# Gated delta-rule attention and top-1 column FFN: the key-product rows laid out by halves for their broadcast, four transfers per half in place of eight

## The chip, the core and the metric

The kernel runs on one core of one Trainium2 chip. The metric is the device time of one execution in microseconds. All arithmetic is in 32-bit floats.

## What is computed

A block of attention with a recurrent state, then a column-routed feed-forward layer, both with layer norms and residuals, over x of shape (4, 2048, 512), with 16 heads of 32 channels. The part that matters here is the recurrence over time:

```
def step(S, inp):
    k_t, q_t, v_t, beta_t, a_t = inp
    S = S * a_t[..., None, None]
    kv_mem = jnp.einsum('bhd,bhde->bhe', k_t, S)
    delta = (v_t - kv_mem) * beta_t
    S = S + k_t[..., :, None] * delta[..., None, :]
    y_t = jnp.einsum('bhd,bhde->bhe', q_t, S)
    return (S, y_t)
```

Each delta depends on all earlier ones of its head. The feed-forward layer sends every token to the best of 16 columns (a 512x128 and a 128x512 product with a gelu between), which needs the tokens sorted by column.

## The kernel before, in words

**Tiling.** The 2048 time positions are cut into 32 tiles of T=64 (all 4 batches at once, 256 tokens), and each tile into NC=2 chunks of C=32 positions. Channels lie on the partitions: 4 groups of 4 heads (HP=4, 32 partitions a head), times 4 batches, make G=16 groups in the free dimension. One `step` of each engine's program works on three tiles at once: `chain` is the recurrence of the present tile, `ahead` the projections, norms and decays of the next, `after` the output projection, the routing and the residuals of the last. The loop body of PE, DVE, ACT and POOL holds two such steps and runs 15 times, with two steps before it and two behind it; SP's loop body holds one step. The order within a step is written out by hand for each engine, and semaphores tie the engines together. A second loop behind this one does the sorted column products.

**The recurrence in a chunk.** Within a chunk the deltas solve a triangular system. Its matrix is Ak: the key products of the chunk times the decay between the two positions (`decay_products`, line 1187 of the profile, on DVE). DVE solves it in two halves of CS=16 positions (`solve_half`). For each of 15 positions t0 of a half it multiplies the known delta into a row of the matrix (line 1213, into Ut) and takes it off the later positions (line 1216), each as two instructions of 8 groups. This is done with all 32 channels of a head on their partitions, so a row of the matrix, which belongs to a head, must stand on all 32 partitions of it. That is done by DMA: SP writes Ak to `pair_rows` in DRAM (line 303), waits until it has landed (line 305), and reads it back broadcast over 32 partitions, head by head, into `pairs[0]` and `pairs[1]`, one buffer for each half (line 312). POOL multiplies `pairs` by beta (`pairs_times_beta`, line 997) and DVE waits for that at line 1204. The second half of a chunk also needs the first half's deltas through PE (`first_half_to_u`, line 456).

**Names.** I write (c,j) for half j of chunk c. POOL multiplies in the order (0,1), (1,0), (1,1) and then (0,0) of the next tile. DVE frees `pairs[j]` at the end of a solve, and SP fetches the next half into it then. PE's other work of a step is mostly 128x128 products (lines 402, 510, 518). `state_to_u` (line 446, waits for the state S at 445) opens a step on PE; `add_to_state` (line 1228) closes it on DVE.

Before, `fetch_pairs(c)` did a whole chunk with all the transfers of both halves:

```
sp.dma_start(pair_rows[c].rearrange("h s r -> (h s) r"), Ak[c][:].rearrange("p t g -> p (t g)")).then_inc(s["rows_out"], 16)
...
for s0, t0 in PIECES:
    for h in range(HP):
        rows = pair_rows[c, h, j * CS + s0:j * CS + s0 + PIECE, (j * CS + t0) * G:(j + 1) * CS * G]
```

`PIECES` is [(0, 0), (8, 8)]: the matrix of a half is triangular, so rows 8 to 15 are read for positions 8 to 15 only.

Of the kernel before, what the change touches and what calls it, by code (L numbers as in the profile page):

```python
# [15 lines left out]
H, DH = 16, 32  # L16
# [28 lines left out]
PIECE = CS // 2  # L45
PIECES = [(0, 0), (PIECE, PIECE)]


TURNS = [
    ("xT", 0), ("xT", 1), ("qk", 0), ("rms", 0), ("alpha",), ("qk", 1), ("rms", 1), ("ss", 0),  # L50
    ("wo", 0), ("wo", 1), ("qk", 2), ("ss", 1), ("G", 0), ("G", 1), ("qk", 3),
    ("ss", 2), ("gate", 0), ("ss", 3), ("gate", 1), ("beta", 0), ("xfT", 0), ("xfT", 1), ("beta", 1), ("hid",),
    ("v", 0), ("logits",), ("v", 1), ("rank",)]
# [20 lines left out]
def sandwich_kernel(nc, x, w_in, wa, dt_bias, a_log, norm_w, wo, bo, col_emb, gw1, gb1, gw2, gb2,  # L74
                    w_cols, b_cols, proj_w, proj_b, ln_g, ln_b,
                    c_sq, c_sel, c_mask, c_iota, c_pad, c_tok, c_row, c_col, out, xs_dram):
    with ExitStack() as ctx:
# [57 lines left out]
        Ak = [sb(f"Ak{c}", [P, C, G]) for c in range(NC)]  # L135
# [4 lines left out]
        pairs = [sb(f"pairs{j}", [P, CS, CS, G]) for j in range(2)]  # L140
# [32 lines left out]
        sel_flat = pairs[0][:].rearrange("p s t g -> p (s t g)")  # L173
# [21 lines left out]
        def in_qr(*shape, dt=F32):  # L195
# [40 lines left out]
            pr_ready Ak_ready rows_out kkq_full kkq_free A_ready kt_ready kd_ready kqd_ready  # L236
# [9 lines left out]
        m_xs, m_wc = ([sem(f"{n}{u}") for u in range(MQ)] for n in ("m_xs", "m_wc"))  # L246
        pairs_free, pairs_in = ([sem(f"{n}{j}") for j in range(2)] for n in ("pairs_free", "pairs_in"))
# [19 lines left out]
        pair_rows = nc.dram_tensor("pair_rows", (NC, HP, C, C * G), F32, kind="Internal").ap()  # L267
# [21 lines left out]
        def _(sp):  # L289
# [10 lines left out]
            def fetch_pairs(c):  # L300
                sp.wait_ge(s["Ak_ready"], 1)
                sp.sem_inc(s["Ak_ready"], -1)
                sp.dma_start(pair_rows[c].rearrange("h s r -> (h s) r"), Ak[c][:].rearrange("p t g -> p (t g)")).then_inc(s["rows_out"], 16)
                sp.wait_ge(s["rows_out"], 16)
                sp.sem_inc(s["rows_out"], -16)
                for j in range(2):
                    sp.wait_ge(pairs_free[j], 1)
                    sp.sem_inc(pairs_free[j], -1)
                    for s0, t0 in PIECES:
                        for h in range(HP):  # L310
                            rows = pair_rows[c, h, j * CS + s0:j * CS + s0 + PIECE, (j * CS + t0) * G:(j + 1) * CS * G]
                            sp.dma_start(pairs[j][DH * h:DH * h + DH, s0:s0 + PIECE, t0:CS, :].rearrange("p s t g -> p s (t g)"),
                                         rows.unsqueeze(0).to_broadcast([DH, PIECE, (CS - t0) * G])).then_inc(pairs_in[j], 16)

# [15 lines left out]

            load_tokens(0)
            load_tokens(1)
            fetch_pairs(0)
            fetch_pairs(1)
            load_tokens(2)
            fetch_pairs(0)
            with sp.Fori(0, NT - 3) as i:
                load_residual(i)
                fetch_pairs(1)
                load_tokens(i + 3)  # L340
                store(i)
                fetch_pairs(0)
            load_residual(NT - 3)
            fetch_pairs(1)
            load_tokens(NT - 1)
            store(NT - 3)
            fetch_pairs(0)
            load_residual(NT - 2)
            fetch_pairs(1)
            store(NT - 2)  # L350
            load_residual(NT - 1)
            store(NT - 1)
# [36 lines left out]
        def _(pe):  # L389
# [59 lines left out]
            def first_half_to_u(c, half):  # L449

                if not half:
                    pe.wait_ge(s["A_ready"], 1)
                    pe.sem_inc(s["A_ready"], -1)
                    pe.wait_ge(s["delT_ready"], 1)
                    pe.sem_inc(s["delT_ready"], -1)
                on_tiles(half, "corr_full", lambda g, q, q_half: pe.matmul(  # L456
                    uk[q, g, CS:C], delT[c][q_half, g, :], Ak[c][q_half, CS:C, g],
                    start=False, stop=True, skip_group_check=True))
# [93 lines left out]
            def step(p, chain, after, ahead):  # L552

# [39 lines left out]

                if chain:
# [20 lines left out]

# [22 lines left out]

# [97 lines left out]
        def _(act):  # L738
# [86 lines left out]
            def step(p, chain, after, ahead):  # L825
# [5 lines left out]
                if ahead:  # L831
# [12 lines left out]

# [10 lines left out]
                if ahead:  # L855
# [18 lines left out]
                def next_gate(hp):  # L874
                    act.wait_ge(s["sg_free"], 1)
                    act.sem_inc(s["sg_free"], -1)
                    link(sigmoid("gate", hp, sg[:]))
                    act.sem_inc(s["gate_ready"], 1)

                if ahead:  # L880
                    next_gate(0)
# [8 lines left out]
                if ahead:  # L890
                    next_gate(1)

                def next_beta(hp):
                    link(sigmoid("beta", hp, flat(unit(beta, hp))))
                    act.sem_inc(bank_free("beta", hp), 1)
                    act.sem_inc(s["beta_ready"], 1)

                if ahead:
# [3 lines left out]
                    next_beta(0)  # L902
# [3 lines left out]
                if ahead:  # L906
                    next_beta(1)
# [12 lines left out]

# [53 lines left out]
        def _(pool):  # L974
# [15 lines left out]
            def pairs_times_beta(c, j):  # L990

                pool.wait_ge(pairs_in[j], 16 * HP * len(PIECES))
                pool.sem_inc(pairs_in[j], -(16 * HP * len(PIECES)))  # L993
                for t0 in range(CS - 1):
                    a = pairs[j][:, t0, t0 + 1:CS, :]
                    t = c * C + j * CS + t0 + 1
                    ins = nc.gpsimd.tensor_tensor(a, a, beta[:, :, t:t + WID[t0]].rearrange("p g t -> p t g"), ALU.mult)  # L997
                ins.then_inc(s["pr_ready"], 1)

            def step(p, chain, after, ahead, added):  # L1000

# [6 lines left out]

# [7 lines left out]

# [20 lines left out]
                if ahead:  # L1037
                    for hp in range(2):
                        pool.wait_ge(s["gT_ready"], 1)
                        pool.sem_inc(s["gT_ready"], -1)  # L1040
                        d = flat(unit(dec, hp))
                        link(nc.gpsimd.tensor_tensor(d, gsb[hp], gT[hp], ALU.subtract))
                        dt = d.rearrange("p (n t) -> p n t", t=C)
                        link(nc.gpsimd.tensor_tensor(dt, dt, mask[:].unsqueeze(1).to_broadcast([P, GU * NC, C]), ALU.add))
                        pool.sem_inc(s["diff_ready"], 1)
# [13 lines left out]

# [91 lines left out]
        def _(dve):  # L1151
# [30 lines left out]
            def decay_products(c):  # L1182
# [4 lines left out]
                link(v.tensor_tensor(Ak[c][:].rearrange("p t g -> p g t"), kkq[:, :, 0, :], d, ALU.mult))  # L1187
# [5 lines left out]
            def solve_half(c, j):  # L1193
# [74 lines left out]
            def choose_columns():  # L1268
# [7 lines left out]
                dve.sem_inc(bank_free("logits"), 1)  # L1276
                dve.wait_ge(s["sig_ready"], 1)
# [12 lines left out]

                dve.wait_ge(s["e_ready"], 1)
# [22 lines left out]
            def step(p, chain, after, ahead):  # L1314
# [13 lines left out]
                if after:  # L1328
                    for hp in range(2):
                        normed_outputs(hp)  # L1330
# [11 lines left out]
                if after:  # L1342
                    for tb in range(TB):
                        dve.wait_ge(s["wo_full"], 1)
                        dve.sem_inc(s["wo_full"], -1)
                        link(v.tensor_tensor(y[:, tb, :], bank("wo", tb), bo_sb[:], ALU.add))
                        dve.sem_inc(bank_free("wo", tb), 1)
                        token_stats(y, tb)
# [5 lines left out]
                if ahead:  # L1354
                    for hp in range(2):
                        dve.wait_ge(s["g_copied"], 1)
                        dve.sem_inc(s["g_copied"], -1)
                        link(v.transpose(gT[hp], gsb[hp]))
# [201 lines left out]
```

## Time and profile before

| | before |
|---|---|
| time, median of 3 runs | 4272.6 us (4265.62 to 4274.22) |
| the profiled execution's own time | 4266.35 us |
| its span | 4264.5 us |
| busy share of the span | PE 75%, DVE 67%, POOL 48%, ACT 29% |
| granted TensorE clock, mean | 0.844 |
| DMA, mean | 91 GB/s |

Times are in us from the start of the span, durations of one instruction in ns where it says so. The two-step loop stands between about 190 and 3520 us; its iterations start some 222 us apart. In a row of the timeline, "[2.64 <-DVEq L1227]" says that the engine had sat idle for 2.64 us before the row and that the wait at line 1227 ended that. "<-issue" is idle time in which the engine waited for nothing that the profile shows. A row that merges n instructions has "xn" at its end; a 32-bit product of PE counts as two.

### The profile page before, as it was taken

To read this page: it belongs to the slowest core of one execution; us is meant where nothing else is said; L and a number is where in the kernel's file an instruction comes from. 1 tells how busy PE (TensorE), PEld (TensorE's weight loads), DVE (VectorE), ACT (ScalarE), POOL (GpSimd) and SP (SyncE) were. 2 spreads that over 40 slices of the span, in tenths; PEclk is the share of its full clock that TensorE was granted. 3 is DMA by queue.
4 is the path that set the end of the run, shared out by engine and by line. 5 is a ranking of instruction groups with operands and counts; after the bars stand their busy time and mean duration, and the time that the engine had idled before them with its cause. 6 is when DMAs were issued, how large, how long until landed. Compare 5 with 4: busy or idle time off the path is not lost. (4 is left out here: it accounts for less than half of the span.)

```text
span 4264.5 us, 151843 instructions
## 1 busy us (share of the span) xinstructions
PE 3206.8 (75%) x59364; PEld 2424.2 (57%) x59364; DVE 2863.6 (67%) x12347; ACT 1247.4 (29%) x2119; POOL 2051.5 (48%) x3051
## 2 busy tenths in 40 slices
PE   5787878888788888887888887888887885355553
PEld 4566656666566666666666666666666664233332
DVE  1676767777776767776777676767777776565655
ACT  2233333333333333333333233333333331111110
POOL 1444444444444444444444444444445443277776
PEclk9898888988888989888988898888898896677766
DMA  4444444433344444444434343434444442466663
GB/s 114 77 86 87 86 86 81 84 73 82 75 85 82 86 86 86 87 86 86 86 77 86 79 89 76 86 75 83 84 86 86 86 86 49 140 151 145 150 150 75
DMA packets 416983, 388.41 MB, mean 91 GB/s; under 512 B 42816, under 2 KB 346560, under 8 KB 415824
## 3 DMA queue, kind: packets, MB, share of 16 engines
q1 hardware_dynamic: 399696, 345.37, 38.0%
q0 software_dynamic: 16640, 33.71, 3.8%
q8 instruction: 492, 8.06, 0.8%
q14 instruction: 155, 1.27, 0.1%
HBM read 307.22 MB, written 75.93 MB: 90 GB/s over the span
## 5 line engine op out<-in xcount | busy, mean ns | idle before, releaser
L402 PE MATMUL work<-xT,w_sb 128*128 128x256 f32 x5120 | 1387.6, 421 | 122.9 <-PEq L393 101.8
L997 POOL TENSOR_TENSOR pairs<-pairs,beta 128x240 f32<-128x240 f32 (+14 forms) x1920 | 938.7, 529 | 982.2 <-POOLq L993 982.2
L402 PEld LDWEIGHTS work<-xT,w_sb 128*128 128x128 f32 x5120 | 1029.4, 209 | 337.1 <-issue 186.1
L1213 DVE TENSOR_TENSOR Ut<-pairs,uk 128x120 f32<-128x120 f32 (+14 forms) x3840 | 833.3, 255 | 25.6 <-DVEq L1204 20.9
L1216 DVE TENSOR_TENSOR uk<-uk,Ut 128x120 f32<-128x120 f32 (+14 forms) x3840 | 708.2, 226 | 0.0
L446 PE MATMUL uk<-kqd,S 32*32 32x32 f32 x8192 | 121.4, 216 | 243.5 <-PEq L445 186.5
L510 PE MATMUL work<-wo_sb,ctxT 128*128 128x512 f32 x512 | 269.6, 687 | 17.2 <-PEq L393 17.2
L1200 DVE TENSOR_TENSOR uk<-vT,uk 128x128 f32<-128x128 f32 x256 | 63.3, 293 | 311.2 <-DVEq L1320 186.2
L986 POOL TENSOR_TENSOR kqd<-kq,eg 128x1024 f32<-128x1024 f32 x64 | 150.5, 2352 | 231.4 <-POOLq L1053 231.4
L446 PEld LDWEIGHTS uk<-kqd,S 32*32 32x32 f32 x8192 | 106.5, 127 | 272.9 <-issue 272.4
L771 ACT ACTIVATE qraw<-work 128x512 f32<-128x512 f32 x128 | 75.9, 593 | 628.2 <-ACTq L770 628.2
L728 PE MATMUL kkq<-w_sb,kq 128*128 128x512 f32 x160 | 130.6, 913 | 104.3 <-PEq L727 104.3
L1034 POOL TENSOR_TENSOR x<-x,y 128x512 f32<-128x512 f32 x64 | 81.3, 1270 | 247.8 <-POOLq L1033 247.8
L510 PEld LDWEIGHTS work<-wo_sb,ctxT 128*128 128x128 f32 x512 | 110.9, 223 | 153.7 <-issue 152.5
L708 PE MATMUL work<-squares,w_sb 128*128 128x128 f32 x320 | 70.2, 367 | 166.7 <-PEq L706 166.4
L708 PEld LDWEIGHTS work<-squares,w_sb 128*128 128x128 f32 x320 | 51.7, 191 | 213.5 <-issue 213.3
L436 PEld LDWEIGHTS kkq<-kq 32*32 32x32 f32 x8192 | 135.3, 115 | 57.5 <-issue 57.5
L464 PE MATMUL uq<-kqd,S 32*32 32x32 f32 x8192 | 102.4, 200 | 83.5 <-issue 83.5
L1135 POOL DMA_INDIRECT out<-pairs,qr x80 | 130.0, 1624 | 72.3 <-POOL pairs L1133 33.7
L956 ACT ACTIVATE kq<-work 128x512 f32<-128x512 f32 x80 | 47.8, 597 | 387.4 <-ACTq L954 387.4
L436 PE MATMUL kkq<-kq 32*32 32x64 f32 x8192 | 156.9, 230 | 4.1 <-issue 4.1
L456 PEld LDWEIGHTS uk<-Ak,delT 16*32 16x32 f32 x8192 | 88.7, 113 | 117.8 <-issue 117.8
(190 smaller groups left out, 5637.7 us busy)
## 6 DMA issues: line engine op xcount, KB each, us to landing
pairs<-pair_rows SPq DMA_DIRECT2D x512, 256.0 KB, 5.0
pairs<-pair_rows SPq DMA_DIRECT2D x512, 128.0 KB, 6.3
w_sb<-xs_rows SPq DMA_DIRECT2D x80, 258.0 KB, 2.8
w_sb<-in_w_cols SPq DMA_DIRECT2D x80, 256.0 KB, 4.1
w_sb<-in_proj_w SPq DMA_DIRECT2D x80, 256.0 KB, 4.3
xt<-in_x SPq DMA_DIRECT2D x66, 256.0 KB, 3.8
pair_rows<-Ak SPq DMA_DIRECT2D x64, 256.0 KB, 2.0
x<-in_x SPq DMA_DIRECT2D x64, 256.0 KB
```

The lines of the kernel that those rows point to most:

```text
L402: mm = pe.matmul(w[:, half * BT:(half + 1) * BT], w_sb[:, f, j * D + hg * P:j * D + (hg + 1) * P], xT[:, f, :], start=(f == 0), stop=(f == ...
L436: on_tiles(half, "kkq_full", lambda g, q, q_half: pe.matmul(kkq[q, g], kq[q, g, c, 0, :], kq[q, g, c].rearrange("p a t -> p (a t)"), start ...
L446: on_tiles(half, "uk_full", lambda g, q, q_half: pe.matmul(uk[q, g], S[q, g, :], kqd[c][q, g, 0, :], start=(g == 0), stop=True, skip_group ...
L464: on_tiles(half, None, lambda g, q, q_half: pe.matmul(uq[q, g], S[q, g, :], kqd[c][q, g, 1, :], start=(g == 0), stop=True, skip_group_chec ...
L510: mm = pe.matmul(w, flat(ctxT[:, hg * B + tb * BL:hg * B + (tb + 1) * BL, :]), wo_sb[:, hg, :], start=(hg == 0), stop=(hg == KD - 1))
L708: mm = pe.transpose(m_tp[u % 2][:, f * P:(f + 1) * P], xs[u][:, f * P:(f + 1) * P], ident)
L728: pe.matmul(m_yp[u % 2], hm[u % 2], pw[u], start=True, stop=True).then_inc(s["m_y"], 1)
L986: link(nc.gpsimd.tensor_tensor(kqd[c][:], kq[:, :, c], eg[:, :, c * C:(c + 1) * C].unsqueeze(2).to_broadcast([P, G, 2, C]), ALU.mult))
L997: ins = nc.gpsimd.tensor_tensor(a, a, beta[:, :, t:t + WID[t0]].rearrange("p g t -> p t g"), ALU.mult)
L1135: nc.gpsimd.indirect_dma_start(out_rows, bass.IndirectOffsetOnAxis(ap=toki[:, u:u + 1].bitcast(U32), axis=0), z[u], None, bounds_check=ROW ...
L1213: link(v.tensor_tensor(Ut[:, g, 0:n], pr[:, g], uk[:, g, at:at + 1].to_broadcast([P, G // 2, n]), ALU.mult), behind=1)
L1216: link(v.tensor_tensor(uk[:, g, at + 1:at + 1 + n], uk[:, g, at + 1:at + 1 + n], Ut[:, g, 0:n], ALU.subtract), behind=1)
```

## The change

`Ak` is laid out as [half, group, position in the half] in place of [position, group]. `pair_rows` has a part for each half, in which the 16 rows of a head stand one behind the other with 16 x 16 floats each. So the 15 rows that a half needs are one run of 15 KB, and a head is one transfer of 32 partitions x 3840 floats: four transfers per half in place of eight. `PIECES` is gone: all 16 positions of all 15 rows are read. `pairs[j]` is [row, group, position]. The instructions that read or write `Ak` and `pairs` are the same in number and size with their strides exchanged. `rows_out` is a semaphore for each chunk. SP's program is written as one `step`, with the write of the rows apart from the two fetches.

```
-        Ak = [sb(f"Ak{c}", [P, C, G]) for c in range(NC)]
+        Ak = [sb(f"Ak{c}", [P, 2, G, CS]) for c in range(NC)]
-        pairs = [sb(f"pairs{j}", [P, CS, CS, G]) for j in range(2)]
+        pairs = [sb(f"pairs{j}", [P, CS, G, CS]) for j in range(2)]
-        pair_rows = nc.dram_tensor("pair_rows", (NC, HP, C, C * G), F32, kind="Internal").ap()
+        pair_rows = nc.dram_tensor("pair_rows", (NC, 2, HP, C, G * CS), F32, kind="Internal").ap()
...
-            def fetch_pairs(c):
+            def write_rows(c):
                 sp.wait_ge(s["Ak_ready"], 1)
                 sp.sem_inc(s["Ak_ready"], -1)
...
+                sp.dma_start(pair_rows[c].rearrange("j h s n -> (h s) j n"), Ak[c][:].rearrange("p j g t -> p j (g t)"))\
+                    .then_inc(rows_out[c], 16)
+
+            def fetch_pairs(c, j):
+                if not j:
+                    sp.wait_ge(rows_out[c], 16)
+                    sp.sem_inc(rows_out[c], -16)
+                sp.wait_ge(pairs_free[j], 1)
+                sp.sem_inc(pairs_free[j], -1)
+                for h in range(HP):
+                    rows = pair_rows[c, j, h, j * CS:j * CS + CS - 1, :].rearrange("s n -> (s n)")
+                    sp.dma_start(pairs[j][DH * h:DH * h + DH, 0:CS - 1].rearrange("p s g t -> p (s g t)"),
+                                 rows.unsqueeze(0).to_broadcast([DH, (CS - 1) * G * CS])).then_inc(pairs_in[j], 16)
...
+            def step(chain, after, ahead, block, following):
+
+                if chain:
+                    fetch_pairs(0, 1)
+                if after:
+                    load_residual(block)
+                if chain:
+                    write_rows(1)
+                    fetch_pairs(1, 0)
+                    fetch_pairs(1, 1)
+                if ahead:
+                    load_tokens(following)
+                if after:
+                    store(block)
+                if ahead:
+                    write_rows(0)
+                    fetch_pairs(0, 0)
...
                 for t0 in range(CS - 1):
-                    a = pairs[j][:, t0, t0 + 1:CS, :]
+                    a = pairs[j][:, t0, :, t0 + 1:CS]
                     t = c * C + j * CS + t0 + 1
-                    ins = nc.gpsimd.tensor_tensor(a, a, beta[:, :, t:t + WID[t0]].rearrange("p g t -> p t g"), ALU.mult)
+                    ins = nc.gpsimd.tensor_tensor(a, a, beta[:, :, t:t + WID[t0]], ALU.mult)
...
-                link(v.tensor_tensor(Ak[c][:].rearrange("p t g -> p g t"), kkq[:, :, 0, :], d, ALU.mult))
+                link(v.tensor_tensor(Ak[c][:].rearrange("p j g t -> p g j t"),
+                                     kkq[:, :, 0, :].rearrange("p g (j t) -> p g j t", j=2),
+                                     d.rearrange("p g (j t) -> p g j t", j=2), ALU.mult))
...
-                    pr = pairs[j][:, t0, t0 + 1:CS, :].rearrange("p t g -> p g t")
+                    pr = pairs[j][:, t0, :, t0 + 1:CS]
```

The rest of the diff writes loops out and splits functions; it leaves the other engines' instructions in their order.

SP's queue in its loop body and just behind it, before (Ak0 and Ak1 are the two chunks, pairs0 and pairs1 the two halves' buffers):

```order
L303 DMA pair_rows<-Ak0 128x512 [waits store_done,Ak_ready]
L312 DMA pairs0<-pair_rows 32x8x256 [waits rows_out,pairs_free0]
L312 DMA pairs0<-pair_rows 32x8x256 x3
L312 DMA pairs0<-pair_rows 32x8x128 x4
L312 DMA pairs1<-pair_rows 32x8x256 [waits pairs_free1]
L312 DMA pairs1<-pair_rows 32x8x256 x3
L312 DMA pairs1<-pair_rows 32x8x128 x4
L337 REGISTER_ALU
L337 COMPARE_AND_BRANCH
L319 DMA x1<-in_x 64x2x512 [waits x1_free]
```

The same place after:

```order
L304 DMA pair_rows<-Ak0 128x2x256 [waits store_done,Ak_ready]
L315 DMA pairs0<-pair_rows 32x3840 [waits rows_out0,pairs_free0]
L315 DMA pairs0<-pair_rows 32x3840 x3
L355 REGISTER_ALU
L355 COMPARE_AND_BRANCH
L315 DMA pairs1<-pair_rows 32x3840 [waits pairs_free1]
L315 DMA pairs1<-pair_rows 32x3840 x3
L322 DMA x1<-in_x 64x2x512 [waits x1_free]
```

Eight issues per half became four; the loop's branch moved from behind the fetch of (0,1) to ahead of it; each transfer follows the same ones as before.

DVE's queue behind the first solve of a step, before:

```order
L1220 STREAM_TRANSPOSE delT0<-uk 128x512 [waits dve_step]
L1323 STREAM_TRANSPOSE kd0<-kq 128x512 [waits dve_step]
L1323 STREAM_TRANSPOSE kd1<-kq 128x512 [waits dve_step]
L1187 TENSOR_TENSOR Ak1<-kkq,dec 128x16x32 [waits dve_step,kkq_full]
L1189 TENSOR_TENSOR Aq1<-kkq,dec 128x512 [waits dve_step]
```

And after:

```order
L1217 STREAM_TRANSPOSE delT0<-uk 128x512 [waits dve_step]
L1322 STREAM_TRANSPOSE kd0<-kq 128x512 [waits dve_step]
L1322 STREAM_TRANSPOSE kd1<-kq 128x512 [waits dve_step]
L1182 TENSOR_TENSOR Ak1<-kkq,dec 128x16x2x16 [waits dve_step,kkq_full]
L1186 TENSOR_TENSOR Aq1<-kkq,dec 128x512 [waits dve_step]
```

Nothing changed its place; the write of Ak has one more dimension.

## Rows read from the trace of the kernel before

**Rows 1.** The page's first line.

```profile
span 4264.5 us, 151843 instructions
```

**Rows 2.** The page's costliest groups: busy us, mean ns of one, idle before.

```profile
L997 POOL TENSOR_TENSOR pairs<-pairs,beta 128x240 f32<-128x240 f32 (+14 forms) x1920 | 938.7, 529 | 982.2 <-POOLq L993 982.2
L1213 DVE TENSOR_TENSOR Ut<-pairs,uk 128x120 f32<-128x120 f32 (+14 forms) x3840 | 833.3, 255 | 25.6 <-DVEq L1204 20.9
L1216 DVE TENSOR_TENSOR uk<-uk,Ut 128x120 f32<-128x120 f32 (+14 forms) x3840 | 708.2, 226 | 0.0
```

**Rows 3.** Groups by line, the two products of decay_products on DVE.

```profile
L1187 DVE TENSOR_TENSOR Ak<-kkq,dec 128x512 f32<-128x512 f32 x64 | 66.1, 1033 | 24.2 <-DVEq L1185 24.2
L1189 DVE TENSOR_TENSOR Aq<-kkq,dec 128x512 f32<-128x512 f32 x64 | 44.2, 691 | 9.4
```

**Rows 4.** The page's DMA issues: count, KB each, median us to landing.

```profile
pairs<-pair_rows SPq DMA_DIRECT2D x512, 256.0 KB, 5.0
pairs<-pair_rows SPq DMA_DIRECT2D x512, 128.0 KB, 6.3
```

**Rows 5.** Busy time in stretches; the last three columns are clock, DMA share, GB/s.

```profile
0.00:20.00 20.00, 0.00 (x0) 0.00 (x0) 0.00 (x0) 0.00 (x0) 0.18 (x4) 1.00 0.84 309
1723.00:1742.00 19.00, 13.55 (x190) 11.23 (x188) 10.98 (x48) 6.35 (x10) 7.79 (x16) 0.86 1.07 194
1767.50:1775.50 8.00, 4.74 (x217) 3.44 (x216) 5.60 (x22) 4.07 (x8) 3.50 (x3) 0.93 1.07 197
1784.00:1788.00 4.00, 4.00 (x16) 2.57 (x15) 3.09 (x6) 0.00 (x0) 0.82 (x4) 1.00 1.14 202
1788.00:1790.00 2.00, 2.00 (x10) 1.58 (x9) 1.66 (x11) 0.26 (x1) 0.00 (x0) 1.00 1.23 192
```

**Rows 6.** Timeline of SP's issues, two chunks of one step.

```profile
1722.60 8.98 SPq L312 DMA_DIRECT2D pairs<-pair_rows  x16
1766.54 19.37 SPq L312 DMA_DIRECT2D pairs<-pair_rows  x16
```

**Rows 7.** Timeline of PE over both steps of one loop iteration.

```profile
1745.15 0.54 PE L446 MATMUL uk<-kqd,S 32*32 32x32 f32 x22 [6.95 <-PEq L445]
1748.21 1.70 PE L446 MATMUL uk<-kqd,S 32*32 32x32 f32 x106 [2.52 <-issue]
...
1776.09 0.87 PE L464 MATMUL uq<-kqd,S 32*32 32x32 f32 x49 [3.85 <-issue]
...
1810.75 0.73 PE L456 MATMUL uk<-Ak,delT 16*32 16x16 f32 x64 [2.17 <-PEq L455]
...
1818.45 3.44 PE L402 MATMUL work<-xT,w_sb 128*128 128x256 f32 x8 [2.85 <-PEq L393]
...
1853.97 1.69 PE L446 MATMUL uk<-kqd,S 32*32 32x32 f32 x92 [4.95 <-PEq L445]
1857.36 0.74 PE L446 MATMUL uk<-kqd,S 32*32 32x32 f32 x36 [1.70 <-issue]
...
1900.37 0.49 PE L478 MATMUL su<-delT,kd 32*32 32x32 f32 x34 [2.76 <-issue]
...
1926.96 3.75 PE L402 MATMUL work<-xT,w_sb 128*128 128x256 f32 x8 [3.99 <-PEq L393]
```

**Rows 8.** Timeline of DVE in the same iteration.

```profile
1740.92 0.69 DVE L1228 TENSOR_TENSOR S<-Sd,su 128x512 f32<-128x512 f32 x1 [0.37 <-DVEq L1227]
...
1766.60 0.19 DVE L1246 TENSOR_TENSOR alog<-work,dtb 128x32 f32<-128x32 f32 x1 [1.57 <-DVEq L1245]
...
1792.85 0.69 DVE L1237 TENSOR_TENSOR kq<-qraw,qr 128x512 f32<-128x512 f32 x1 [2.44 <-DVEq L1236]
...
1901.13 0.69 DVE L1228 TENSOR_TENSOR S<-Sd,su 128x512 f32<-128x512 f32 x1 [2.64 <-DVEq L1227]
```

**Rows 9.** Timeline of POOL in the same iteration.

```profile
1732.60 7.23 POOL L997 TENSOR_TENSOR pairs<-pairs,beta 128x240 f32<-128x240 f32 x15 [26.01 <-POOLq L993]
...
1871.32 1.08 POOL L1012 TENSOR_TENSOR kd<-kd,dec 128x512 f32<-128x512 f32 x1 [1.38 <-POOLq L1010]
```

More of the change, by code:

```diff
@@ L246, in sandwich_kernel @@
         m_xs, m_wc = ([sem(f"{n}{u}") for u in range(MQ)] for n in ("m_xs", "m_wc"))
+        rows_out = [sem(f"rows_out{c}") for c in range(NC)]
         pairs_free, pairs_in = ([sem(f"{n}{j}") for j in range(2)] for n in ("pairs_free", "pairs_in"))
@@ L594, in step @@
                     first_half_to_u(0, 1)
-                if chain:
                     state_to_outputs(0, 0)
@@ L890, in step @@
                 if ahead:
[L891 to L898, printed above, removed]
+                    act.wait_ge(s["sg_free"], 1)
+                    act.sem_inc(s["sg_free"], -1)
+                    link(sigmoid("gate", 1, sg[:]))
+                    act.sem_inc(s["gate_ready"], 1)
                     if chain:
@@ L901, in step @@
                         act.sem_inc(s["vb_free"], -1)
-                    next_beta(0)
+                    link(sigmoid("beta", 0, flat(unit(beta, 0))))
+                    act.sem_inc(bank_free("beta", 0), 1)
+                    act.sem_inc(s["beta_ready"], 1)
                 if after:
@@ L906, in step @@
                 if ahead:
-                    next_beta(1)
+                    link(sigmoid("beta", 1, flat(unit(beta, 1))))
+                    act.sem_inc(bank_free("beta", 1), 1)
+                    act.sem_inc(s["beta_ready"], 1)
                 if after:
@@ L1328, in step @@
                 if after:
-                    for hp in range(2):
-                        normed_outputs(hp)
+                    normed_outputs(0)
+                    normed_outputs(1)
                 if ahead:
@@ L1342, in step @@
                 if after:
[L1343 to L1348, printed above, removed]
+                    dve.wait_ge(s["wo_full"], 1)
+                    dve.sem_inc(s["wo_full"], -1)
+                    link(v.tensor_tensor(y[:, 0, :], bank("wo", 0), bo_sb[:], ALU.add))
+                    dve.sem_inc(bank_free("wo", 0), 1)
+                    token_stats(y, 0)
+                    dve.wait_ge(s["wo_full"], 1)
+                    dve.sem_inc(s["wo_full"], -1)
+                    link(v.tensor_tensor(y[:, 1, :], bank("wo", 1), bo_sb[:], ALU.add))
+                    dve.sem_inc(bank_free("wo", 1), 1)
+                    token_stats(y, 1)
                     token_norm(rstd, nmr, s["norm_ready"])
@@ L1354, in step @@
                 if ahead:
[L1355 to L1358, printed above, removed]
-                        dve.sem_inc(s["gT_ready"], 1)
+                    dve.wait_ge(s["g_copied"], 1)
+                    dve.sem_inc(s["g_copied"], -1)
+                    link(v.transpose(gT[0], gsb[0]))
+                    dve.sem_inc(s["gT_ready"], 1)
+                    dve.wait_ge(s["g_copied"], 1)
+                    dve.sem_inc(s["g_copied"], -1)
+                    link(v.transpose(gT[1], gsb[1]))
+                    dve.sem_inc(s["gT_ready"], 1)
                 if chain:
```

110 lines of the change are left out of this document (47 added, 63 removed).

## The prediction

> **What bounds the kernel now.** The page gives a span of 4264.5 us [rows 1]; the profiled execution took 4266.35 us, 1.85 us outside the span. That is inside the runs shown (4265.62 to 4274.22) and 6.2 us under their median, so I make the sum against 4266.35 and read the result against 4272.6. What can be told from no change here is about 0.2%, 8.5 us.
>
> After the page I read the waits, because no engine is full. POOL's largest wait is for the broadcast itself: 982 us before its products on pairs [rows 2]. It is tempting to take that for the price of the transfers. But DVE, which consumes those products, waited for POOL only 20.9 us in the whole span (the releaser in its row in rows 2). So a pairs transfer that lands earlier releases nobody: POOL's products of (0,0) end at 1739.8 [rows 9] and DVE's next solve begins only after PE's products, which end at 1749.9 [rows 7].
>
> Then the timelines of PE and DVE over one loop iteration, for who waits for whom. Two kinds of stretches take turns.
> - PE waits for DVE: 2.17 us for the deltas of solve (1,0) and 2.85 us for a bank that DVE frees behind it in the first step, 3.99 us for the same bank in the second [rows 7]. Solve (1,0) is on the path in both steps. In the second step solve (0,1) is too, as far as PE's next product waits for DVE's work behind it.
> - DVE waits for PE: 1.57 us behind solve (0,0), 2.44 us behind solve (0,1) of the first step [rows 8]. There a faster DVE waits longer.
>
> The third finding is the one that decides. PE also stands where the profile shows nobody to wait for: 3.85 us at 1776, 2.52 us at 1748, 1.70 us at 1857, 2.76 us at 1900 [rows 7]. And at the head of the loop body, S is ready at 1741.6 [rows 8] but PE begins at 1745.15, 3.5 us later [rows 7]. I read these as PE's instructions not being there yet: they fall in runs of many small products, one after the other. They go with the broadcast: the transfers of (1,0) end at about 1775.3 (the stretch to 1775.5 runs at 197 GB/s, rows 5) and PE goes on at 1776.09. The broadcast of both (0,j) fills 1723 to 1742 [rows 5], and PE's late start follows it. So the transfers are on the path after all, through how long they keep the DMA engines full, not through their landing.
>
> **DVE's gain.** Line 1213 reads pairs with a step of 64 bytes, after the change with none. Its 3840 instructions take 833.3 us, those of line 1216, of the same sizes and without such a step, 708.2 us [rows 2]. Over 128 halves that is 6.51 and 5.53 us: 0.98 us less per solve if 1213 falls to 1216's cost. The write of Ak shows the same effect: 1033 ns with the step, 691 ns for its twin Aq without [rows 3], 0.34 us less. Bounds for a solve: 0 and 0.98 us; I take 0.98, since the Ak/Aq pair is alike in all but the step.
> On the path stand two solves (1,0) per pair of steps: 2 x 0.98 = 1.96 us. The second step's (0,1) gives up to 0.98 us more, which the term below on (1,1) takes back. The other five solves and both Ak lie beside PE's work [rows 8]; if that cover went they would be worth 0.98 us each.
>
> The Trainium skill, SBUF — State Buffer (Door 1: The DMA port swizzle), states 16-byte lines in SBUF, with a penalty for every access to a new one. The pair of rows on Ak and Aq agrees.
>
> **The transfers.** Before, a half is 4 x 256 KB + 4 x 128 KB = 1.57 MB [rows 4]. After, it is 4 x 480 KB = 1.97 MB, 25% more. How fast will it go? While runs of 1 KB move (1784 to 1788) the rate is 202 GB/s; while those of 512 B move (1788 to 1790) it is 192 [rows 5]. Twice the runs for the same bytes cost 5%, so it is mostly bytes and not their number that sets it. With 15 KB I expect 205 GB/s. The other bound is 309 GB/s, the first 20 us, with runs of up to 10 KB to all 128 partitions [rows 5]; I take the near row, because the destinations are still 32 partitions. A half then takes 9.6 us in place of 7.9, and with 199 GB/s 9.9: I use +1.9 us. Two halves back to back: +3.8 us. What that touches:
> - The (0,j) transfers start 0.98 + 0.34 = 1.3 us sooner, since DVE's solve and Ak are shorter, and end 3.8 - 1.3 = 2.5 us later against PE. Their end was 1742, before PE's start at 1745.15; in the second step PE's gap ends at 1857.36 [rows 7]. Each of these two starts can move by 0 (if the instructions wait for something else) to 2.5 us. I take the middle, 1.25 us each: +2.5 us.
> - (1,0), first step: starts 1.3 us sooner, lasts 1.9 longer; PE goes on 0.6 us later: +0.6 us.
> - (1,1), second step: starts 0.98 us sooner behind (0,1), ends 0.9 us later. PE's gap up to 1900.37 ends with it, and DVE waits there for PE (2.64 us at 1901, rows 8): +0.9 us, and the solve's gain is swallowed.
> Sum +4.0 us per pair of steps; bounds 0 and 2 x 2.5 + 0.6 + 0.9 = 6.5.
>
> Which way do instructions and data share a DMA engine? The gap that ends at 1776.09, right behind the burst, speaks for waiting. The Trainium skill, DMA: Bandwidth & Descriptors (Queues, rings and completion order), says that an engine takes turns between queues packet by packet; by that the length of a burst would cost PE nothing, and the sum would be the solves alone, 4219 us. Its section on back-pressure, told for transfers between cores, says that stalled writes hold up an engine's other queues; by that the whole 2.5 us would come each time, and 4339 us.
>
> **SP.** Its order stays. The number of issues falls from 16 to 8 per chunk; they took 8.98 us for a burst of 15 us and more [rows 6], so they were covered, and the gain is nothing. If the cover went (transfers faster than issues) it would be half a microsecond each. The branch between (0,0) and (0,1) stands behind a (0,0) that takes over 9 us: covered.
>
> **POOL.** Products per half: 7.23 us [rows 9]. After, they are 16 short rows each in place of one run, and beta is read without a step. No row has rows as short as 1 to 15 elements. Below: line 997 could fall by a fifth. Above: it could take 12 us. Behind (0,0) and (0,1) POOL waits only 1.38 us before kd in the second step [rows 9], but PE's products with kd stand at 1900 [rows 7], over 20 us later. I take nothing, and from about 5 us per half on it would cost.
>
> **PE.** Line 456 reads Ak without a step now; its 64 records take 0.73 us [rows 7]. I take no change.
>
> **Sum.** -1.96 + 4.0 = +2.0 us per pair, 16 pairs (32 steps have a chain): +33 us, 4266.35 + 33 = 4299. The second loop's instructions are the same. Bounds with the same solves: (-1.96 + 0) x 16 = -31 us, 4235; (-1.96 + 6.5) x 16 = +73 us, 4339; with no gain on DVE 4370.
>
> **The rivals.**
> - *Long runs go faster.* At 309 GB/s a half takes 6.4 us, 1.5 less than now. The (0,j) end 3.0 + 1.3 = 4.3 us sooner, of which PE's late start can use 3.5 at most and the gap of 1.70 all; the gap at 1776 gives 2.8, that at 1900 about 2. With the solves up to 12 us per pair; the waits for ranks and projections take about half of that as they close up. I say 5 us: 4266 - 80 = 4186. The startup row speaks for it, the like rates of 1 KB and 512 B against it. It decides from about 250 GB/s on, where a half takes as long as now. Chance 0.18.
> - *Bursts don't matter, strides do.* PE's gaps are their own (branch and small products), and all three solves on the path pay: 16 x 2.94 = 47 us: 4219. For it: at 1748 a gap of 2.52 us stands with no transfer near. Chance 0.17.
> - *The change washes out.* Terms within 0.5 us per pair: 4258 to 4275. Chance 0.13.
> - *Worse than the sum.* At 205 GB/s over 16 engines a 15 KB run holds an engine for 1.2 us, a 1 KB run for 0.08, and every fetch of instructions waits for it, in stretches where PE has no gap today too. At 2 us for each of four gaps on top: 4299 + 128 = 4427. Nothing in the trace shows such a run beside PE's small products. Chance 0.07, half of it over 4370.
> - *The forecast:* 4281 to 4345, chance 0.45.
>
> **How the numbers follow.** Slower by over 0.2%: 0.45 + 0.07 = 0.52. Within: 0.13. Faster: 0.18 + 0.17 = 0.35. The forecast's own range is 4281 to 4345. The range 4200 to 4350 leaves out most of the first rival and the worst case, about 2 in 10.
>
> **What the profile after would show.** Line 1213 at about 710 us of busy time and Ak at 691 ns (else the strides were not the price). Transfers of 480 KB at about 205 GB/s and bursts of 19 us for (0,j) (at 250 or more the first rival holds). PE's start at the loop's head later than 3.5 us behind S, and its gaps behind 1776 and 1900 no shorter. POOL's products under 12 us per half, and still nearly no wait of DVE at line 1204. I am wrong in the main if PE's gaps shrink though the bytes grow, or if they stay as they are.

## The result and the profile after

The changed kernel takes 4320.9 us (median, 4316.0 to 4329.3), the kernel before 4273.4 on the same chip: ratio 1.0117, 95% interval 1.0094 to 1.014, so 1.2% slower. The profiled execution has a span of 4314.2 us against 4264.5 [rows 1]. The forecast was 4299.

The page's groups, as in [rows 2, 3]:

```profile
span 4314.2 us, 151331 instructions
...
L990 POOL TENSOR_TENSOR pairs<-pairs,beta 128x240 f32<-128x240 f32 (+14 forms) x1920 | 837.2, 475 | 998.7 <-POOLq L986 998.7
...
L1182 DVE TENSOR_TENSOR Ak<-kkq,dec 128x512 f32<-128x512 f32 x64 | 44.3, 692 | 27.7 <-DVEq L1180 27.7
L1210 DVE TENSOR_TENSOR Ut<-pairs,uk 128x120 f32<-128x120 f32 (+14 forms) x3840 | 690.1, 216 | 22.4 <-DVEq L1201 17.7
```

Every engine is busy for less time or as long. The solve's products (line 1210, before 1213) fall from 833.3 to 690.1 us busy, 1.12 us per half, Ak from 1033 to 692 ns, POOL's products from 938.7 to 837.2 us; PE is busy 3179.9 us for 3206.8. Yet the kernel is slower, so the place to look is idle time, and first that of PE. The waits of PE, largest first (us in total, times, longest), of the kernel before and then of the changed one; lines 446, 464, 478 of before are 453, 471, 485 after:

```profile
PE uk L446 <- PEq L445: 186.5, 32, 8.6
...
PE uq L464 <- issue: 83.5, 33, 4.1
PE uk L446 <- issue: 56.8, 28, 3.1
...
PE su L478 <- issue: 32.0, 13, 3.0
```

```profile
PE uq L471 <- issue: 190.5, 33, 7.1
PE uk L453 <- PEq L452: 189.1, 32, 9.9
...
PE uk L453 <- issue: 84.0, 32, 4.9
...
PE su L485 <- issue: 11.8, 8, 3.0
```

One row carries it: PE's wait before uq<-kqd,S, with nothing to wait for that the profile shows, grows by 107 us, 6.7 per pair of steps. DVE's wait before `vT - uk` (line 1197, 223.9 us) and the others follow it. PE at that place in a first step of an iteration, and SP's two fetches in the same step:

```profile
1797.57 0.73 PE L463 MATMUL uk<-Ak,delT 16*32 16x16 f32 x64
1798.17 0.86 PE L471 MATMUL uq<-kqd,S 32*32 32x32 f32 x79
1805.90 0.86 PE L471 MATMUL uq<-kqd,S 32*32 32x32 f32 x49 [6.88 <-issue]
```

```profile
1746.64 3.95 SPq L315 DMA_DIRECT2D pairs<-pair_rows  x8
...
1793.08 16.59 SPq L315 DMA_DIRECT2D pairs<-pair_rows  x8
```

After 79 of the 128 products PE stops. In [rows 7] the same place (1776.09) has 3.85 us. The transfers now, in stretches of both (0,j) and of (1,0) (clock, DMA share, GB/s last):

```profile
1747.50:1766.00 18.50, 15.06 (x197) 12.86 (x195) 7.92 (x38) 6.22 (x10) 6.45 (x15) 0.91 1.02 213
1793.00:1802.50 9.50, 6.03 (x222) 4.17 (x222) 6.30 (x29) 4.07 (x8) 3.48 (x3) 1.00 0.94 207
```

So 1.97 MB take 9.5 us at 207 GB/s, as forecast (205).

**What PE waits for.** The DMA view of a short stretch says which queues moved packets in it (packets, MB, busy share of 16 engines). From 1802.5 to 1804.5, right behind the burst, it has

```profile
q8 instruction: 1, 0.02, 4.5%
```

one packet of the instruction queue, 4.5% of 16 engines over 2 us, or 1.44 us of one engine; from 1797.0 to 1802.5 there is none. The packet starts between 1803.0 and 1803.5 and PE goes on at 1805.90. No view says for which engine a packet is; that it is PE's is read from the times. In ten such places, in seven of the kernels of this document, with gaps from 0.2 to 6.9 us, PE goes on 2.0 to 3.4 us behind the packet's start. The whole program has 492 such packets and 8.06 MB in both kernels, 16 KB each.

### The profile page after: what moved, and what is told of

It reads as the page before. It is cut to its first block and busy times, and to the rows that moved or that the text cites. A ratio compares the mean times of both kernels' runs of the same rounds, so it can differ in the third digit from the quotient of the medians.

```text
span 4314.2 us, 151331 instructions
## 1 busy us (share of the span) xinstructions
PE 3179.9 (74%) x59364; PEld 2414.0 (56%) x59364; DVE 2690.5 (62%) x12347; ACT 1245.7 (29%) x2119; POOL 1951.0 (45%) x3051
## 3 DMA queue, kind: packets, MB, share of 16 engines
q8 instruction: 492, 8.06, 0.8%
## 5 line engine op out<-in xcount | busy, mean ns | idle before, releaser
L409 PE MATMUL work<-xT,w_sb 128*128 128x256 f32 x5120 | 1346.2, 411 | 139.4 <-PEq L400 119.5
L990 POOL TENSOR_TENSOR pairs<-pairs,beta 128x240 f32<-128x240 f32 (+14 forms) x1920 | 837.2, 475 | 998.7 <-POOLq L986 998.7
L409 PEld LDWEIGHTS work<-xT,w_sb 128*128 128x128 f32 x5120 | 1003.5, 204 | 338.0 <-issue 197.0
L1210 DVE TENSOR_TENSOR Ut<-pairs,uk 128x120 f32<-128x120 f32 (+14 forms) x3840 | 690.1, 216 | 22.4 <-DVEq L1201 17.7
L453 PE MATMUL uk<-kqd,S 32*32 32x32 f32 x8192 | 120.4, 216 | 273.1 <-PEq L452 189.1
L517 PE MATMUL work<-wo_sb,ctxT 128*128 128x512 f32 x512 | 288.9, 728 | 4.4 <-PEq L400 4.4
L1197 DVE TENSOR_TENSOR uk<-vT,uk 128x128 f32<-128x128 f32 x256 | 63.2, 293 | 332.8 <-DVEq L1319 223.9
L471 PE MATMUL uq<-kqd,S 32*32 32x32 f32 x8192 | 110.2, 208 | 190.5 <-issue 190.5
L471 PEld LDWEIGHTS uq<-kqd,S 32*32 32x32 f32 x8192 | 96.4, 120 | 214.9 <-issue 214.9
L1234 DVE TENSOR_TENSOR kq<-qraw,qr 128x512 f32<-128x512 f32 x128 | 93.0, 727 | 124.1 <-DVEq L1233 124.1
```

The costliest lines, as they stand in the source:

```text
L409: mm = pe.matmul(w[:, half * BT:(half + 1) * BT], w_sb[:, f, j * D + hg * P:j * D + (hg + 1) * P], xT[:, f, :], start=(f == 0), stop=(f == ...
L453: on_tiles(half, "uk_full", lambda g, q, q_half: pe.matmul(uk[q, g], S[q, g, :], kqd[c][q, g, 0, :], start=(g == 0), stop=True, skip_group ...
L471: on_tiles(half, None, lambda g, q, q_half: pe.matmul(uq[q, g], S[q, g, :], kqd[c][q, g, 1, :], start=(g == 0), stop=True, skip_group_chec ...
L517: mm = pe.matmul(w, flat(ctxT[:, hg * B + tb * BL:hg * B + (tb + 1) * BL, :]), wo_sb[:, hg, :], start=(hg == 0), stop=(hg == KD - 1))
L1210: link(v.tensor_tensor(Ut[:, g, 0:n], pr[:, g], uk[:, g, at:at + 1].to_broadcast([P, G // 2, n]), ALU.mult), behind=1)
```

## The experiments

The question behind all of them: the burst got 25% more bytes and runs of 15 KB in place of 1 KB, fewer transfers, and it starts at another time against PE. Which of these holds up the instructions? Every run was timed against the kernel before on its own chip, whose median was between 4265 and 4290 us; so the ratios are compared, and a ratio is turned into microseconds with 4273.

**Bytes or long runs.** runs_1k parts the rows in DRAM by 64 numbers, for the write and for the fetch, and changes nothing else (theory B is that the extra bytes lengthen PE's waits for instructions, theory L that the long runs do):

```
-pair_rows = nc.dram_tensor("pair_rows", (NC, 2, HP, C, G * CS), ...)
+pair_rows = nc.dram_tensor("pair_rows", (NC, 2, HP, C, G * CS + 64), ...)
...
-rows = pair_rows[c, j, h, j * CS:j * CS + CS - 1, :].rearrange("s n -> (s n)")
+rows = pair_rows[c, j, h, j * CS:j * CS + CS - 1, 0:G * CS]
```

> The changed kernel with each row of the broadcast 64 numbers apart in DRAM, so that the same 1.97 MB per half go in runs of 1 KB instead of 15 KB (15 times the packets, the same four transfers, the same tiles and engines' work). Theory B (the extra bytes lengthen PE's waits for instructions): about 4321 us, and the idle time before the product uq<-kqd,S stays at 190 us. Theory L (it is the long run, which holds an engine while the instruction fetch stands behind it): 4240 to 4270 us, and that idle time falls to about 85 us, its value in the kernel before.

Ratio 1.011, interval 1.0088 to 1.0132. The run length is worth nothing in the time; theory L is out. The wait before uq is 24 us less than the 190.5 that B wanted, which the time doesn't show:

```profile
PE uq L471 <- issue: 166.6, 33, 6.4
```

The next two fetch fewer rows (`j * CS + 12` in place of `j * CS + CS - 1`, and one memset at the start), with long and with short runs. They leave out rows 12 to 14, which stay zero, so they don't compute the block.

> The changed kernel with only rows 0 to 11 of each half fetched: runs of 12 KB, 1.57 MB per half, as many bytes as in the kernel before. Rows 12 to 14 of each half are left out (they stay zero from the start), the engines' instructions are the same. Theory B: 4225 to 4240 us, since the bursts are as short as before and DVE's gain is left; idle time before uq<-kqd,S about 85 us. Theory L: 4290 us or more, the idle time still 150 us or more.

> The same 12 rows (rows 12 to 14 of each half left out), but in runs of 1 KB: the bytes of the kernel before, its run length, and the changed layout in SBUF. Theories B and L both: 4225 to 4240 us. It is the reference for the pair: B wants it equal to the 12 KB runs, L wants it 50 us or more below them.

Ratios 0.9821 (0.9785 to 0.9858) and 0.9835 (0.9797 to 0.9872), 4196 and 4203 us, 20 to 30 us below what B said. Against their twins with 15 rows (1.0117 and 1.011) the 0.4 MB per half are worth 2.96% and 2.75%, 126 and 118 us. Both have four transfers per half, and the engines do the same work in all four, so this is the price of bytes. The zeros don't shorten the second loop: from its first write of `xs_rows` to the end of the span it is 603 us in rows12_long, 605 in the changed kernel. The waits before uq, long and short:

```profile
PE uq L471 <- issue: 124.9, 33, 5.6
```

```profile
PE uq L471 <- issue: 141.9, 33, 6.0
```

They are above the 83.5 us of the kernel before with as many bytes. B had said 85; I come back to it.

before_full goes the other way, the old layout with the whole half:

```
-for s0, t0 in PIECES:
-    for h in range(HP):
-        rows = pair_rows[c, h, j * CS + s0:j * CS + s0 + PIECE, (j * CS + t0) * G:(j + 1) * CS * G]
+for h in range(HP):
+    rows = pair_rows[c, h, j * CS:j * CS + CS - 1, j * CS * G:(j + 1) * CS * G]
```

> The kernel before, with the whole half of 15 rows and 16 columns fetched by one transfer per head (1.97 MB per half instead of 1.57, runs of 1 KB, 4 transfers instead of 8), its strides of 64 bytes kept. Theory B: 4340 to 4370 us, the bytes' cost (about 100 us) without DVE's gain of 30 us and more. Theory L: 4275 to 4290 us, since no long run is in it.

Ratio 1.0364 (1.0339 to 1.0389), 4429 us: 59 us above the range of B. Over the kernel before it is 155 us, 30 us and more above what the same bytes cost in the changed layout. B left out that this edit also makes four transfers of eight.

**No burst.** row1_only sends one row of 15; the others are left out and stay zero.

> The changed kernel with only row 0 of each half fetched (one run of 1 KB per partition, 0.13 MB per half; rows 1 to 14 are left out and stay zero), all engines' instructions unchanged. It shows what the bursts cost in all. Theory B (the fetch of PE's instructions stands behind the burst on the DMA engines): 3950 to 4080 us, and the idle time before uq<-kqd,S falls from 190 us to under 40 us. Rival, from my prediction (PE's gaps are its own, a fetch that comes at that place whatever else moves): that idle time stays at 80 us or more and the time is 4150 us or more.

Ratio 0.9358 (0.9335 to 0.9381), and the wait before uq goes from 190.5 to 14.1 us:

```profile
PE uq L471 <- issue: 14.1, 23, 2.2
```

So "PE's gaps are its own" is out for this gap. The same place in its timeline, and the DMA view from 1647.0 to 1648.0:

```profile
1648.02 0.72 PE L463 MATMUL uk<-Ak,delT 16*32 16x16 f32 x64
1648.61 0.86 PE L471 MATMUL uq<-kqd,S 32*32 32x32 f32 x79
1650.00 0.62 PE L471 MATMUL uq<-kqd,S 32*32 32x32 f32 x49 [0.53 <-issue]
```

```profile
q8 instruction: 1, 0.02, 5.7%
```

Without a burst the packet takes 0.9 us of an engine (5.7% of 16 us) and starts up to half a microsecond ahead of the second product on Ak (1648.02); in the changed kernel it starts 5.4 to 5.9 us behind it, in the first stretch in which the burst is through. PE's program is the same, so I take it that the packet is asked for at the same place (no view shows the asking), and that the burst holds it. It doesn't always hold it to its end: at another place of the changed kernel (below) the packet starts between 1685.0 and 1685.5 while the burst moves data until about 1687.5, and in the kernel before it starts between 1773.0 and 1773.5 with the burst running until about 1775.5. In runs_1k it starts between 1574.0 and 1574.5, 4.6 to 5.1 us behind the second product on Ak (1569.41), although the packets ahead of it are of 1 KB:

```profile
1577.14 0.87 PE L471 MATMUL uq<-kqd,S 32*32 32x32 f32 x49 [6.28 <-issue]
```

The Trainium skill, DMA: Bandwidth & Descriptors (Queues, rings and completion order), lets an engine change between queues behind every packet. Even if a packet were all that one transfer has on an engine (30 KB, 2.4 us at 207 GB/s over 16 engines), the fetch should have come sooner than 5 us late; these traces don't agree.

**Which solves are on the path.** Three more DVE instructions behind a solve, in all four of a step, or in (1,0) alone:

```
 dve.wait_ge(dve_step, link.n)
+if (c, j) == (1, 0):                      # delay_10; in delay_all always
+    for _ in range(3):
+        link(v.tensor_tensor(Ut[:, :, 0:CS - 2], Ut[:, :, 0:CS - 2], Ut[:, :, 0:CS - 2], ALU.subtract))
 dve.sem_inc(pairs_free[j], 1)
```

> The changed kernel with three more DVE instructions (some 1.2 us, about what the stride cost a solve) behind the last of each solve, in all four solves of a step, before the pairs are given free. Theory W (what the layout is worth sits in the three solves on the path and a later start of the transfers): 60 to 100 us more than the changed kernel. Theory of my prediction (two solves (1,0) on the path per pair of steps, the others hidden): 35 to 40 us more.

> The same delay in solve (1,0) alone. My prediction has this solve on the path in every step: 32 x 1.2 = 38 us more than the changed kernel. Rival: it only moves the burst of the next half against PE's fetches, and the difference is under 15 us or over 60.

Ratios 1.031 (1.0284 to 1.0337) and 1.0186 (1.0163 to 1.0209), over the changed kernel's 1.0117 by 1.93% (82 us) and 0.69% (29 us). The groups give 1.45 and 1.31 us per solve, delay_all first:

```profile
L1218 DVE TENSOR_TENSOR Ut<-Ut 128x224 f32<-128x224 f32 x384 | 185.6, 483 | 22.9
```

```profile
L1218 DVE TENSOR_TENSOR Ut<-Ut 128x224 f32<-128x224 f32 x96 | 41.9, 436 | 5.7
```

Per pair of steps the two delays of (1,0) cost 1.8 us of 2.6, all eight 5.1 us of 11.6, as much as 3.5 solves. So (1,0) does pay, less than in full (29 us for the 38 expected), and the other six are not free: together they cost 3.3 us of 8.7. These prices are not those of the solve alone, since a later end of a solve also moves the next burst.

**Fewer bytes, with the whole computation.** blocks sends rows 8 to 14 with their columns 8 to 15 alone:

```
+link(v.tensor_tensor(At[c][:].rearrange("p j g t -> p g j t"),
+                     kkq[:, :, 0, :].rearrange("p g (j t) -> p g j t", j=2)[:, :, :, HS:CS],
+                     d.rearrange("p g (j t) -> p g j t", j=2)[:, :, :, HS:CS], ALU.mult))
...
+for rows, at in ((pair_rows[c, j, h, j * CS:j * CS + HS, :].rearrange("s n -> (s n)"), 0),
+                 (tail_rows[c, j, h, j * CS + HS:j * CS + CS - 1, :].rearrange("s n -> (s n)"), HS * G * CS)):
+    n = rows.shape[0]
+    sp.dma_start(pairs[j][DH * h:DH * h + DH].rearrange("p s g t -> p (s g t)")[:, at:at + n],
+                 rows.unsqueeze(0).to_broadcast([DH, n])).then_inc(pairs_in[j], 16)
```

DVE writes those columns a second time (one more instruction per chunk), and they have rows of their own in DRAM.

> The whole computation, the changed layout, but rows 8 to 14 of a half are sent with their columns 8 to 15 alone: DVE writes those columns of Ak a second time to a tile of their own (one more instruction per chunk), they get their own rows in DRAM, and each head's transfer is one run of 8 KB and one of 3.5 KB. 1.47 MB per half (1.97 after, 1.57 before), 8 transfers per half instead of 4. Theory B: 4180 to 4230 us, 1 to 2% under the kernel before, since 12 rows of 1 KB with 1.57 MB stood at 0.9835 of it. Rival (the number of rows or of transfers counts, not the bytes): 4300 us or more.

Ratio 0.9643 (0.9617 to 0.9669), 4121 us, 59 us below the range of B and 4.7% under the changed kernel. The wait before uq is 56.5 us. Three things moved at once: 1.47 MB, eight transfers where rows12_1k has four, and a later start of the burst in the second steps (see the next part).

**The start of the burst, in runs already made.** In the second steps the same kernel has short and long gaps before uq, and they go with how long SP's first issue for (1,0) stands ahead of the second product on Ak. The kernel before, 15 second steps of the loop: 2.8 to 2.9 us ahead in twelve, with gaps of 0.7 to 1.5 us; 4.4 to 4.6 us ahead in three, with gaps of 3.5 to 3.7 us, for example

```profile
1209.24 3.77 SPq L312 DMA_DIRECT2D pairs<-pair_rows  x8
...
1213.67 0.74 PE L456 MATMUL uk<-Ak,delT 16*32 16x16 f32 x64
...
1218.38 1.70 PE L464 MATMUL uq<-kqd,S 32*32 32x32 f32 x106 [3.72 <-issue]
```

The changed kernel is 3.6 to 5.5 us ahead in all 15, with gaps of 4.4 to 7.1 us; of the shift, the shorter solve (0,0) and the shorter write of Ak ahead of the fetch give up to 1.4 us (an estimate: 10.1 less 9.05 us, as below, and 1033 less 692 ns):

```profile
1677.93 1.71 SPq L315 DMA_DIRECT2D pairs<-pair_rows  x4
...
1681.67 0.73 PE L463 MATMUL uk<-Ak,delT 16*32 16x16 f32 x64
...
1688.38 1.70 PE L471 MATMUL uq<-kqd,S 32*32 32x32 f32 x106 [5.74 <-issue]
```

delay_all has the same bytes, runs and transfers, and a solve (0,0) that ends later. Nine of its 14 second steps are 2.7 us ahead, with gaps of 1.8 to 2.6 us; the other five, 3.3 to 4.2 us ahead, have 4.1 to 7.0 us. Its whole wait before uq is 151.1 us for 190.5. One of the nine:

```profile
1729.12 1.71 SPq L315 DMA_DIRECT2D pairs<-pair_rows  x4
...
1731.84 0.73 PE L463 MATMUL uk<-Ak,delT 16*32 16x16 f32 x64
...
1735.14 1.10 PE L471 MATMUL uq<-kqd,S 32*32 32x32 f32 x106 [2.32 <-issue]
```

before_full has the old starts with 1.97 MB in four transfers: 2.9 us ahead in twelve of 14, its gaps are 2.0 to 2.9 us. So bytes and fewer transfers alone give a little over 1 us per second step, and the rest goes with the earlier start, which DVE's own gain brings about. No run parts the two in the time.

**When the burst starts, on purpose.** hold_10 keeps all bytes and transfers of the changed kernel and has SP wait ahead of (1,0):

```
+if (c, j) == (1, 0):
+    sp.wait_ge(s["outs_sent"], 1)      # PE's last product uq<-kqd,S of chunk 0
+    sp.sem_inc(s["outs_sent"], -1)
 sp.wait_ge(pairs_free[j], 1)
```

> The changed kernel, bytes and transfers as they are, but SP holds the transfers of (1,0) until PE has sent the last product of uq<-kqd,S of chunk 0; they start some 6 us later than now, behind the fetch of instructions instead of ahead of it. Theory B (a fetch of instructions that is asked for during a burst comes when the burst is through): the idle time before uq<-kqd,S falls from 190 us to under 40 us, and the time by 60 to 150 us, to 0.975 to 1.0 of the kernel before. Rival (each burst costs what it lasts, wherever it stands): the wait turns up before another product, and the time stays at 1.01 of the kernel before or rises.

Ratio 0.9999 (0.9982 to 1.0016): all of the loss is gone, 1.2% or 50 us, a little less than the 60 that B asked for. The waits:

```profile
PE uk L456 <- PEq L455: 249.9, 57, 10.0
...
PE uk L456 <- issue: 96.3, 47, 3.8
...
PE uq L474 <- issue: 10.9, 20, 2.2
```

The wait before uq is 10.9 us, as without a burst. Of these 180 us 73 turned up before uk<-kqd,S (249.9 and 96.3 for 189.1 and 84.0), as the rival said. This is the run that shows what the waits come from: same bytes, same runs, same transfers; the order of burst and fetch differs, and what follows on the later start. It doesn't show that all of the change's loss came from this place: the kernel before has 83.5 us of the same wait, and what the hold is worth there was not tried.

> The same hold in the version with rows 8 to 14 cut to their columns 8 to 15 (1.47 MB per half), where the idle time before uq<-kqd,S is 56 us. Theory B: that idle time falls under 30 us, and the time to 0.95 to 0.965 of the kernel before. Rival: 0.965 or more, since the burst of (1,0) and (1,1) now end later and the fetches of the next products wait for them.

Ratio 0.9595 (0.9569 to 0.9622), 4100 us, the fastest version found, with the wait before uq at 8.9 us. It is half a per cent under blocks, whose interval it just overlaps, and 5.2% under the changed kernel.

The second hold has SP wait ahead of (0,1) too (`if (c, j) == (0, 1)`, on a semaphore that PE raises behind `state_to_u(0, 1)`).

> The changed kernel with the hold of (1,0) as before and a second one: SP holds the transfers of (0,1) until PE has gone past its products uk<-kqd,S of chunk 0 at a step's head, so that only those of (0,0) run ahead of them. Theory B: PE's late start there (uk<-kqd,S idle 346 us in hold_10 in its two forms) shrinks by 80 us or more, and the time to 0.975 to 0.995 of the kernel before. Rival (PE starts late there for S and for its own branch, or (0,1) then comes too late for DVE's solve): no less than 0.9999.

> Both holds in the version with rows 8 to 14 cut to their columns 8 to 15. Theory B: 0.940 to 0.956 of the kernel before. Rival: no less than 0.9595, the value with the first hold alone.

Ratios 1.0105 (1.0074 to 1.0137) and 0.9666 (0.9641 to 0.9691): both slower than with one hold, and B's times were wrong. Against the changed kernel (1.0117) hold_both is no different within the intervals. The waits of PE in hold_both, and one of DVE:

```profile
PE uk L459 <- PEq L458: 180.3, 59, 5.4
...
PE kkq L449 <- issue: 105.4, 32, 5.7
...
PE uk L459 <- issue: 63.7, 69, 2.7
```

```profile
DVE Ak L1189 <- DVEq L1187: 148.2, 64, 8.1
```

The late start did shrink, by 102 us in its two forms (346.2 to 244.0), as B said. But the burst of (0,1) now stands over PE's key products, which wait 105.4 us for their instructions and had waited 3.0 us in hold_10, and DVE's Ak, which the next rows are written from, waits for them: 148.2 us, in hold_10 and the changed kernel under 30. The same mechanism, at a worse place.

## Why the prediction was right, and where its terms were not

**What bounds the kernel.** Right. The transfers are on the path through how long they fill the DMA engines and not through their landing: POOL's wait for pairs reaches 1235 us in hold_10 while the kernel gets 50 us faster. The strongest evidence is hold_10, not the changed kernel.

**DVE's gain** was put at -1.96 us per pair, two solves of 0.98. A solve, from its product with beta to its transpose, went from about 10.1 to 9.05 us, and the busy time says 1.12. The size was right; the claim that only (1,0) pays was not. With the 3.5 solves' worth of delay_all, an estimate, a solve's 1.03 us is 3.6 us per pair, 58 us in all in place of 31. Measured for the layout at 1.57 MB: 0.9835, so -70 us, which holds also POOL's and Ak's share and the step from eight transfers to four. What failed is that the other solves were put at nothing, the second step's (0,1) as taken back by the term on (1,1): that term came out the other way.

**The transfers.** 205 GB/s forecast, 207 measured. A half takes 9.5 us for 7.9, so +1.6; the +1.9 used lay above what 205 GB/s gives, which is 9.6 less 7.9, or +1.7. The term was +4.0 us per pair, 64 us; the bytes cost 118 to 126. By its parts:
- The late starts, +2.5: S is written from 1767.78 to 1768.47 and PE begins at 1773.31, 4.8 us behind it in place of 3.5, so 1.3 where 1.25 was taken. Both rows of line 453 together grew from 243.3 to 273.1 us, 1.9 per pair where +2.5 was put. About right.

```profile
1767.78 0.69 DVE L1225 TENSOR_TENSOR S<-Sd,su 128x512 f32<-128x512 f32 x1 [0.37 <-DVEq L1224]
```

```profile
1773.31 0.54 PE L453 MATMUL uk<-kqd,S 32*32 32x32 f32 x22 [8.49 <-PEq L452]
```

- (1,0), +0.6, first step only: this is the term that failed. Measured +6.7 per pair. The gap is 6.3 us on average in the first steps (3.7 before) and 6.1 in the second ones (1.7 before), twelve gaps each. In the first I reckoned with the burst's end alone, and the packet starts up to 2.5 us ahead of that end in the kernel before. The second, in which [rows 7] shows no gap of note before uq, I did not cost at all. There the packet started between 1876.5 and 1877.0 in the kernel before, some 2 us behind SP's first issue of the burst (1874.71, eight issues over 4.81 us); in the changed kernel, at 1685.0 to 1685.5, it is over 7 us behind it (1677.93, four issues in 1.71 us). The fetch that used to slip in near the start of the burst now stands behind most of it. That PE would wait in stretches where it had no gap stood in the rival "worse than the sum", which put it down to long runs; runs_1k shows it without them.
- (1,1), +0.9: the wait before su<-delT,kd fell by 20 us, -1.3 per pair. Wrong in sign.

A gap costs once more behind itself. The 16 products on wo_sb that follow uq took 9.40 us behind the 6.20 us gap at 1579.74, in a stretch with a granted clock of 0.76, and 7.10 us in hold_10 without that gap, at 1.00:

```profile
1580.50:1590.00 9.50, 9.50 (x27) 4.22 (x19) 5.17 (x22) 0.00 (x0) 6.46 (x15) 0.76 0.73 159
```

```profile
1660.80:1668.00 7.20, 7.17 (x18) 3.35 (x19) 7.04 (x50) 0.00 (x0) 0.00 (x0) 1.00 1.05 220
```

Over the run this group is busy 288.9 us, 269.6 before and 252.9 in hold_10.

**SP, POOL, PE.** POOL's short rows take 6.54 us per half for 7.33, and DVE still waits for it only 17.7 us: nothing, as taken. The same holds for PE's line 463. That fewer issues are worth nothing is in doubt. They were covered, but issues spread over 4.8 us also leave the fetch less to stand behind. This could explain three misses: rows12_1k waits 141.9 us before uq with the bytes of before, before_full cost 30 us more than its bytes should, and blocks with eight transfers did better than its bytes. For the first and the last the start of the burst is a rival: rows12_1k has the changed kernel's shorter solve, and blocks issues its burst only 2.3 us ahead of the second product on Ak in a second step (1806.47 against 1808.77). No run changes the number of transfers alone, so it stays open.

**The sum** of +33 us came close to the +48 measured because two terms, each about half its size, partly cancelled: -31 for -70, +64 for +118. That is partly luck. (Both measured terms are taken at rows12_1k, which stands between the two kernels, so they add up to 48 by construction.) The direction rests on what the prediction had right: more bytes keep PE waiting for instructions, and that outweighs DVE's gain. The rivals: long runs do not go faster (207 GB/s, and runs_1k equal); "bursts don't matter" is out by row1_only; a held engine by long runs is out by runs_1k; and a change that washes out is outside the interval of 1.0094 to 1.014.

## What to carry to other kernels

Where PE stands with "issue" in a run of small products, look in the DMA view of that stretch for the packet of the instruction queue, and at which burst it follows. Then ask for each bulk transfer not only what waits for it but which fetch stands behind it: here the same bytes, held 6 us or so by one semaphore, were worth 1.2%, and a second hold at another place took as much away. When a change makes the work ahead of a burst shorter, the burst starts sooner too: look whether that puts it ahead of a fetch. A price read from a gap in one kind of step says nothing on the steps in which the burst and the fetch come in the other order: look at both before the change moves one of them.

## What was not expected of the hardware

- A fetch of 16 KB that starts up to 0.5 us ahead of the second product on Ak without a burst (row1_only) started 5.4 us or more behind it with 1.97 MB of queued transfers in runs of 15 KB, and 4.6 us or more with runs of 1 KB. In the time, the size of the packets ahead changes nothing (1.0117 and 1.011). By what rule the engines put it at or near the burst's end was not tried.
- Bursts cost this kernel 0.9358 against 1.0117: 324 us, 7.5%, while only POOL waits for their data (998.7 us), and DVE waits 17.7 us for POOL.
- With the same bytes and transfers, a burst issued 2.7 us ahead of the second product on Ak left gaps of 1.8 to 2.6 us, and one issued 3.3 to 4.2 us ahead left 4.1 to 7.0 us (delay_all).
- Broadcasts to 32 partitions ran at 207 GB/s with runs of 15 KB against 202 and 192 with 1 KB and 512 B [rows 5].
